# GpSimd subtracts two tiles at once and takes two residual sums; SyncE's queue and the first batch in another order

## What is computed

```python
x = x + layernorm(attention(layernorm(x)))
x = x + layernorm(ffn(layernorm(x)))

# attention, 16 heads of 8 columns, 512 positions
q, v = x @ Wq.T + bq, x @ Wv.T + bv
bits = ([q, 1] @ hyperplanes) >= 0                  # 6 bits, so 64 buckets
scores = q @ q.T / sqrt(128)
coeff = 62 + (bucket[s] == bucket[t])
out = softmax(scores * coeff) @ v

# feed-forward, 128 -> 512 -> 512 -> 512 -> 128, weights of -1, 0, 1 with a scale per output
h = silu(x @ w1 * s1) * (x @ w2 * s2)
h = gelu(h @ h1 * s);  h = gelu(h @ h2 * s);  out = h @ w3 * s3
```

## Time and profile before

| | us |
|---|---|
| median of three runs | 1542.07 (1539.42 to 1546.05) |
| the profiled execution, its own time | 1544.71 |
| its span in the profile | 1542.9 |
| first coefficients of batch 0 | at 40.42 |
| last tile of batch 0, of batch 15 | at 115.8, at 1454.6 |
| TensorE, VectorE busy | 1366.8, 1341.6 |
| GpSimd, ScalarE busy | 1241.5, 1184.0 |

### The profile page before, as it was taken

How to read it: one execution, slowest core, us unless ns; L and a number is a source line. 1 busy time by engine, 2 the same in 40 slices (tenths; PEclk the granted TensorE clock), 3 DMA queues, 4 the chain that set the end, 5 groups by cost and what they waited for, 6 DMA issues and landing times. The chain is left out here.

```text
span 1542.9 us, 22812 instructions
## 1 busy us (share of the span) xinstructions
PE 1366.8 (89%) x6502; PEld 630.4 (41%) x6624; DVE 1341.6 (87%) x4058; ACT 1184.0 (77%) x1587; POOL 1241.5 (80%) x1177
## 2 busy tenths in 40 slices
PE   2667899999989999898989989899998989899896
PEld 1222344353444434343443434444353444434343
DVE  3999999999999999999998989899999999898620
ACT  2465878888888888788888877878888788788731
POOL 1799988889888988888887888888889888888810
PEclk9987999999999999999999999999999999999999
DMA  2522321223132222312221221322213232222000
GB/s 59 151 70 66 76 64 53 70 47 87 44 77 72 60 62 60 81 36 76 73 70 50 57 75 47 76 69 51 72 43 84 52 76 66 52 61 57 16 0 14
DMA packets 145230, 95.44 MB, mean 62 GB/s; under 512 B 102608, under 2 KB 134608, under 8 KB 145104
## 3 DMA queue, kind: packets, MB, share of 16 engines
q1 hardware_dynamic: 145104, 93.97, 24.0%
HBM read 83.21 MB, written 10.75 MB: 61 GB/s over the span
## 5 line engine op out<-in xcount | busy, mean ns | idle before, releaser
L900 POOL TENSOR_TENSOR logits<-max_row,logits 128x512 f32<-128x512 f32 x912 | 1139.7, 1283 | 161.0 <-ACT max_row L930 156.3
L707 DVE CUSTOM_DVE_ANT_0 logits<-s_bank,coeff 128x512 f32<-128x512 f32 x1024 | 698.6, 682 | 0.2 <-issue 0.2
L688 DVE TENSOR_SCALAR coeff<-brow,bcol 128x516 bf16<-128x516 bf16 x1024 | 482.7, 471 | 70.3 <-PE s_bank L489 24.9
L939 ACT ACTIVATE probs<-logits 128x1024 f32<-128x1024 f32 x512 | 525.0, 1054 | 8.3 <-POOL logits L900 7.3
L489 PE MATMUL s_bank<-mov_stack,stat_stack 128*128 128x512 bf16 x902 | 325.9, 394 | 105.0 <-DVE rowmax L707 39.1
L489 PEld LDWEIGHTS s_bank<-mov_stack,stat_stack 128*128 128x128 bf16 x1024 | 95.6, 98 | 452.1 <-issue 206.7
L930 ACT COPY max_row<-s_bank 128x512 f32<-128x512 f32 x256 | 148.6, 580 | 166.4 <-PE s_bank L497 166.3
L518 PE MATMUL aux_bank<-probs,v_pad 128*32 128x512 f32 x2048 | 265.8, 615 | 6.8 <-issue 3.9
L622 PE MATMUL f_bank<-hid_a,h_sb 128*128 128x512 f32 x512 | 243.0, 596 | 14.1 <-DVE hid_a L805 12.1
L632 PE MATMUL f_bank<-hid_b,h_sb 128*128 128x512 f32 x512 | 249.3, 600 | 1.6 <-ACT hid_b L1014 1.4
L497 PE MATMUL s_bank<-ident,rowmax 128*128 128x128 f32 x1024 | 159.5, 280 | 8.0 <-issue 2.4
(11 more groups left out here) (83 smaller groups left out, 1132.7 us busy)
## 6 DMA issues: line engine op xcount, KB each, us to landing
brow<-bucket_scratch SPq DMA_DIRECT2D x64, 516.0 KB
mov_stack<-q_scratch SPq DMA_DIRECT2D x64, 288.0 KB
stat_stack<-q_scratch SPq DMA_DIRECT2D x192, 96.0 KB
q_scratch<-q_parts SPq DMA_DIRECT2D x48, 128.0 KB, 3.5
x_in<-in_x SPq DMA_DIRECT2D x16, 256.0 KB, 10.4
x_res<-in_x SPq DMA_DIRECT2D x16, 256.0 KB, 2.8
out<-ffn SPq DMA_DIRECT2D x16, 256.0 KB, 2.3
h_sb<-in_h1T SPq DMA_DIRECT2D x1, 1024.0 KB, 8.5
```

The lines of the kernel that those rows point to most:

```text
L688: nc.vector.tensor_scalar(coeff[:, k % 3, :].rearrange("p (r n) -> p r n", r=ROW_RUNS), brow[:, h // 4 % 2, h % 4, :, 0:RUN], bcol[:, b % ...
L707: nc.vector.tensor_tensor_reduce(out=logits[:, k % RING, :], in0=tile_bank(k)[:], in1=coeff[:, k % 3, 0:SEQ], scale=float(E) ** -0.5, scal ...
L900: nc.gpsimd.tensor_tensor(logits[:, k % RING, :], max_row[:, h % 2, :], logits[:, k % RING, :], ALU.subtract).then_inc(below_max_done, 1)
L939: nc.scalar.activation(probs[:, h // 4 % 2, h % 4, t:t + 2, :], logits[:, k % RING:k % RING + 2, :], ACT.Exp, scale=-1.0).then_inc(probs_d ...
```

## The change

GpSimd takes two neighbouring tiles of a head in one instruction, with `max_row` read twice. In the seven heads where VectorE takes the fourth tile, GpSimd takes a pair and a single tile. Both residual sums move from VectorE to GpSimd in the same slots. `apart` goes. SyncE's queue is written as a loop over slots: the store of q (now two DMAs, five parts in all, c0 c1 c2 c0 c1) stands in slot 1, the load of x in slot 2, the store of the bucket rows in slot 39 and `x_res` in slot 40; `mov_stack` is loaded in three DMAs of 24 rows and `stat_stack` in three of 24 rows that are read in a rotated order; the bucket rows are kept in DRAM with the pitch that they have in SBUF. For batch 0 the projections use PSUM banks of their own and fewer waits, and the query projection of batch 1 moves into slots 2 to 8 of batch 0.

```diff
+            for parts, row in ((PARTS, 0), (PARTS - 1, PARTS * DH)):
+                sp.dma_start(q_scratch[p][row:row + parts * DH, :].rearrange("(c d) (h n) -> (d h) c n", d=DH, h=H),
+                             q_parts[:, 0:parts, :]).then_inc(q_written, 16)
...
-                sp.dma_start(mov_stack[0:KROWS, slot].rearrange("p h n -> p (h n)"),
-                             q_scratch[b][:, cols].unsqueeze(0).broadcast_to([PARTS, PARTS * DH, 4 * SEQ])
-                             ).then_inc(stack_loaded[slot], 16)
                 for i in range(PARTS):
                     rows = slice(i * PARTS * DH, (i + 1) * PARTS * DH)
+                    sp.dma_start(mov_stack[rows, slot].rearrange("p h n -> p (h n)"),
+                                 q_scratch[b][0:PARTS * DH, cols]).then_inc(stack_loaded[slot], 16)
                     sp.dma_start(stat_stack[rows, slot].rearrange("p h n -> p (h n)"),
-                                 q_scratch[b][i * DH:(i + 1) * DH, cols].unsqueeze(0).broadcast_to(
-                                     [PARTS, DH, 4 * SEQ])).then_inc(stack_loaded[slot], 16)
+                                 q_scratch[b][i * DH:(i + PARTS) * DH, cols]).then_inc(stack_loaded[slot], 16)
...
                 if k == V_SLOT:
-                    pe.wait_ge(bits_done, p + 1)
+                    if begun(p):
+                        pe.wait_ge(bits_done, p + 1)
...
                 if k == PROJ_SLOT:
                     pe.wait_ge(q_done, p + 1)
-                    pe.wait_ge(q_part_steps, 4 * (p + 1))
+                    if begun(p):
+                        pe.wait_ge(q_part_steps, 4 * (p + 1))
...
-                if k == RESIDUAL_SLOT:
-
-                    dve.wait_ge(normed_done, f + 1)
-                    dve.wait_ge(x_res_loaded, 16 * (f + 1))
-                    nc.vector.tensor_tensor(y1[:, f % 2], y1[:, f % 2], x_res[:], ALU.add).then_inc(y1_done, 1)
...
                 h, t = divmod(k, ST)
-                if t == 0:
+                first = k - 1 if t % 2 else k
+                n = k - first + 1
+                if t < 2:
                     pool.wait_ge(max_row_done, b * H + h + 1)
                 pool.wait_ge(logits_done, b * TILES + k + 1)
-                nc.gpsimd.tensor_tensor(logits[:, k % RING, :], max_row[:, h % 2, :], logits[:, k % RING, :],
+                tiles = logits[:, first % RING:first % RING + n, :]
+                nc.gpsimd.tensor_tensor(tiles, max_row[:, h % 2, :].unsqueeze(1).broadcast_to([P, n, SEQ]), tiles,
                                         ALU.subtract).then_inc(below_max_done, 1)
...
+                    if feed and k == RESIDUAL_SLOT:
+
+                        pool.wait_ge(normed_done, f + 1)
+                        pool.wait_ge(x_res_loaded, 16 * (f + 1))
+                        nc.gpsimd.tensor_tensor(y1[:, f % 2], y1[:, f % 2], x_res[:], ALU.add).then_inc(y1_done, 1)
+                    if finish and k == Y2_SLOT:
+
+                        pool.wait_ge(end_normed_done, g + 1)
+                        nc.gpsimd.tensor_tensor(ffn[:], ffn[:], y1[:, g % 2], ALU.add).then_inc(y2_done, 1)
```

More of the change, by code:

```diff
@@ L43 @@
 PARTS = 3
+ROTATED = 2 * PARTS - 1
 KROWS = PARTS * PARTS * DH
@@ L49 @@
 PADDED = ROW_RUNS * RUN
+ROW_PITCH = ROW_RUNS * RUN_PITCH
 EPS = 1e-5
@@ L123 @@
 S_BANKS = 4
+Q_STORE_SLOT = 1
+FIRST_XNT_SLOT = 2
+FIRST_Q_STORE_SLOT = 11
+X_LOAD_SLOT = 2
+ROW_STORE_SLOT = 39
+X_RES_SLOT = 40
+OUT_SLOT = 63
 SHARED_HEADS = (0, 1, 5, 6, 8, 12, 15)
@@ L316, in maxima_bank, with projection_bank @@
             return s_bank[(k + (k + 1) // ST - 1) % S_BANKS]
-        POOL_TILES = TILES - len(SHARED_HEADS)
-        def pool_tiles(k):
-            return sum(not by_vector(n) for n in range(k + 1))
+        def projection_bank(p, n):
+            return aux_bank if begun(p) else f_bank[n]
         def quads_at(i, k, lag, attend, feed):
@@ L331, in quads_at, with query_at @@
             return []
+        def query_at(i, k, query):
+            steps = []
+            if query and not (i == -1 and k >= XNT_SLOT):
+                steps.append((i + 2, k))
+            if i == 0 and FIRST_XNT_SLOT <= k < FIRST_XNT_SLOT + TILES - XNT_SLOT:
+                steps.append((1, k - FIRST_XNT_SLOT + XNT_SLOT))
+            return steps
         def begun(b):
@@ L401, in iteration @@
                 p, b, f, g = i + 1, i, i - 1, i - 2
-                if query and project and not attend:
-                    sp.wait_ge(xnT_psum, p + 1)
-                    apart(sp)
-                    sp.dma_start(x_in[:], x_view[p + 1]).then_inc(x_loaded, 16)
-                if attend:
-                    if begun(b):
-                        sp.wait_ge(logits_done, b * TILES)
-                        apart(sp)
-                    load_stacks(b, 1)
-                    if query:
+                for k in range(TILES):
+                    if attend and k % QT == 0 and k // QT + 1 < QUADS:
+                        quad = k // QT + 1
+                        if begun(b) or quad > 1:
+                            sp.wait_ge(logits_done, b * TILES + (quad - 1) * QT)
+                        load_stacks(b, quad)
+                    if project and k == (FIRST_Q_STORE_SLOT if i == 0 else Q_STORE_SLOT):
+                        store_query(p)
+                    if query and project and k == (FIRST_Q_STORE_SLOT - 2 if i == 0 else X_LOAD_SLOT):
@@ L447, in iteration @@
-                if project:
-                    if attend:
-                        sp.wait_ge(logits_done, b * TILES + 3 * QT)
-                        apart(sp)
-                    load_stacks(p, 0)
-                if finish:
-                    store_output(g)
+                    if project and k == ROW_STORE_SLOT:
+                        store_row(p)
+                        if not attend:
+                            sp.wait_ge(q_written, 16 * Q_DMAS * (p + 1))
+                            sp.wait_ge(stacks_clear, 3)
+                            load_parts(p, 0)
@@ L456, in _ @@
+                    if finish and k == OUT_SLOT:
+                        store_output(g)
             stages(sp, iteration)
@@ L664, in iteration @@
                         transpose_output(b, quad)
-                    if query:
-                        query_step(i + 2, k, attend)
+                    for p, slot in query_at(i, k, query):
+                        query_step(p, slot, p > 1)
                     if project:
@@ L718, in moments @@
                     dve.wait_ge(stats_done, n)
-                    apart(dve)
                     for t in range(ST):
@@ L730, in output_step @@
                     dve.wait_ge(rden_done, b * QUADS + quad + 1)
+                    if quad == 0 and b:
+                        dve.wait_ge(normed_done, b)
                     nc.vector.tensor_tensor(
@@ L859, in iteration @@
                         project_step(i + 1, k)
-                    if query:
-                        query_step(i + 2, k)
+                    for p, slot in query_at(i, k, query):
+                        query_step(p, slot)
                     if finish:
```

117 lines of the change are left out of this document (55 added, 62 removed).

## The result

The changed kernel takes 1501.39 us (median of 4 runs, 1500.63 to 1502.52) against 1544.06 in the runs of before beside it (1539.42 to 1550.77): a ratio of 0.972, 95% interval 0.968 to 0.976. That is 42.7 us where 22.5 were forecast: the time lies at the lower edge of the range of 1501 to 1537, and outside the forecast's own 1511 to 1529. The runs of before lie 11 us apart, those of after 2; that turns out to matter.

A forecast was written before the change was run, and what follows sets the result against it. VectorE was taken to bound each batch's first half and TensorE the second; minus 18.8 (stalls), minus 4.3 (start) and plus 0.6 (end) gave minus 22.5, so 1519.5 us, range 1501 to 1537.

The forecast's parts named there:

- The stall of quad 3: VectorE's wait for quad 3's DMA load at its first coefficient in each batch; loading it ahead of `x_res` would remove it.
- The pairs: GpSimd's subtractions of two tiles at once: 2.38 us each forecast, valued at nothing for the end of the program.
- The sums: Two residual sums leaving VectorE in the half where TensorE sets the pace: value nothing, bound 2.9 us a batch.
- The wait of the statistics for GpSimd's sum: New wait of VectorE's statistics in slot 23: 0.35 us idle forecast, nothing to pay and no gain.
- The end: Last sum, on the path that ends the program, takes 1.28 in place of 0.69: plus 0.6 us.
- the term of minus 18.8: Steady batches: VectorE's waits for quad 3 in 15 batches go, each counted one for one, minus 18.8 us.
- The rival's sign: Rival on TensorE's clock: a denser TensorE is granted less clock, four more slow batches cost 10 us, 1530; chance 0.12.
- the saving of a pair: GpSimd: each of 25 pairs a batch saves about 0.17 us against two single subtractions, about 4 us less.
- The start: Ahead of the first tile: first coefficients at 33.1 in place of 40.4, minus 7.3 us; net minus 4.3 with batch 0.
- the early bound: Start: earliest case for the first tile, 29, with loads starting at 22.5 and 2 us to land.
- batch 1's q steps: Query projection steps of batch 1, now in slots 5 and 6 of batch 0: plus 3 us (1.4 to 5).
- The 4.9: Start: stacks moving at the full DMA rate land in 2.5 us in place of 7.4, 4.9 us less.

The follow-up runs named there:

- b_quad3_first: The kernel before, with only SyncE's queue reordered so that quad 3 is loaded ahead of the wait and load of `x_res`: 1516.11 us against 1540.63.
- a_single_tiles: The changed kernel with GpSimd subtracting tile by tile instead of in pairs, both residual sums left on GpSimd: 1503.33 us, ratio 0.975 to the kernel before.
- a_sums_vector: The changed kernel with both residual sums moved back from GpSimd to VectorE: 1502.97 us, ratio 0.975 to the kernel before.
- b_copy: The kernel before, run once more unchanged for a second profile: 1541.39 us.
- a_old_stack_loads: The changed kernel with mov and stat stacks loaded in the old form (three copies as outermost dimension), new queue order kept: 1506.42 us, ratio 0.978.

## Why the prediction was too small

**Right.** The stall of quad 3 goes, by the order of SyncE's queue alone (b_quad3_first). The pairs cost 2.37 us and the steady batch doesn't feel them (a_single_tiles). The sums are worth 0.16 us in a steady batch (a_sums_vector), near the nothing of the sum and far from its bound of 2.9. The wait of the statistics for GpSimd's sum is 0.15 or nothing in the steady batch, 0.35 forecast. The direction and the reason for the stall's going hold.

The end, 0.7 more where 0.6 was forecast, came out right by luck. The 0.6 is the last sum alone; by a_sums_vector the sums on GpSimd cost 2.8 there, and some other part of the change gives 2.1 back. Which one, no run shows. In after's chain of work that ended last, GpSimd's output sum stands ahead of its last subtractions, for which ScalarE's exponential waits until 1421.13:

```profile
1411.69 1.27 POOL ffn L921
1412.96 8.17 POOL logits L899 x4
1421.13 0.02 issue
1421.15 1.06 ACT probs L951
```

That delay of the batch behind it was no term of the sum.

**The step that failed** is the term of minus 18.8: "the stall adds to the batch one for one". It measured minus 28.1 in b_quad3_first. The 9.3 beyond the stalls can be laid out by batch, each less its stall against the same batch of b_quad3_first. The five with a dip behind their stall took 1.8, 2.9 and 2.9 more in the middle, and 1.6 and 1.5 in the last two (86.28 and 86.71 against 84.72 and 85.23), 10.7 in sum. The nine others from batch 2 on took 0.12 to 0.17 each, 1.3 in sum, which no dip explains. Batch 1 took 2.7 less (82.07 against 84.79); it has 84.82 in the second profile of before, so this is a difference between executions and not the queue's. Against that second profile (b_copy, three dips) batches 1 to 15 give 24.4, 18.7 of them stalls, which is near the 24.5 of the medians: the profile on which the forecast rested was a costly one. I had taken one for one from two batches and took the second for its long stall, 1.82, without looking at the clock behind it; it happened to be one of two long stalls without a dip. The batches near 825 to 1010 that took 91 to 92.5 were in my text, but as a rival: that a denser TensorE would be granted less clock. It was the other way about. The clock fell where TensorE had stood idle, so a change that fills its idle time wins the clock as well. The rival's sign was wrong, and those three batches were part of the gain. A smaller slip: the earlier trace rows call the wait that ends at 636.93 TensorE's last for VectorE before 691, but one of 0.21 ends at 637.53; it changes nothing. Nor does the saving of a pair, which by the prediction's own 2.57 and 2.38 is 0.19 and not 0.17.

The Trainium skill, in TensorE: Matmul & The Clock Gate, section "What's actually happening", says that the default state is throttled and activity releases it. Our rows agree in direction: 0.57 behind 2.14 us idle, 0.50 behind 4.92, 0.60 behind 3.36. That sentence gives the rival the other sign.

**The rest of the 35.5** is 7.4: 3.7 in batches 1 and 2, and 3.7 in batches 3 to 15, or 0.3 each in most (87.89 to 87.59). Of these 0.3 the sums are 0.16; the other 0.15 I can't assign to an edit. Batch 2 goes with the sums too: it takes 89.17 to 89.31, less the stall, in b_quad3_first and in both profiles of before, 89.81 in a_sums_vector, which keeps the new first batch, and 87.66 in after. So 1.5 more came from a term that the sum put at nothing. Why batch 2 gains more than a steady batch is open. Batch 1, of which TensorE runs a part at the low clock, takes 82.07 and 84.82 in the two profiles of before; its 2.2 can't be assigned.

In all the span fell 20.8 us further than forecast: 9.3 by the stalls' term, 7.4 by the rest of the batches, 4.2 by the start and batch 0.

**The start** gave 9.9 where I had 7.3, because two terms were mis-sized. SyncE's queue from 22.13, in after, shows the loads behind the store of the rows at 21.68 (22.1 forecast):

```profile
21.68 0.34 SPq L413 DMA_DIRECT2D bucket_scratch<-brow  x1
22.13 0.36 SPq L391 DMA_DIRECT2D mov_stack<-q_scratch  x1
...
24.52 0.35 SPq L400 DMA_DIRECT2D brow<-bucket_scratch  x1
```

Issue was over at 24.87 in place of 28.7: loads started 0.4 us ahead of the early bound, and the six took 2.35 us in place of the 4.3 at 0.72 each. Landing then took 5.65, more than the 4.4 that I had left. Batch 0 took 1.4 us more, the least of the 1.4 to 5 allowed for batch 1's q steps. No run takes these steps out, and the mean granted clock over batch 0 is 0.87 in after and 0.93 in before, so that they are the cause is not shown.

How many engines carry a load of 24 rows was the question on which I cited the Trainium skill. The window of after while such loads run, and below it the same microsecond of a_old_stack_loads, with the old form (DMA share before last, GB/s last):

```profile
24.00:25.00 1.00, 0.00 (x0) 0.00 (x0) 0.00 (x0) 0.00 (x0) 0.84 (x3) 1.00 0.75 184
```

```profile
24.00:25.00 1.00, 0.00 (x0) 0.00 (x0) 0.00 (x0) 0.00 (x0) 0.84 (x3) 1.00 0.19 45
```

0.75 of 16 is 12 engines, and 0.19, as in the earlier trace rows, is three. The rule of the Trainium skill, in DMA: Bandwidth & Descriptors, section on why a DMA increments its semaphore by 16 and not by 1, gives the same two numbers. The 4.9 that the prediction took from the rates in the earlier trace rows for this measured 5.2 (a_old_stack_loads).

## What to carry over

In this kernel a wait on the path had two prices: its length, and what TensorE lost behind it when its clock fell. Before pricing a stall, list every batch with its length less its stall and the granted clock behind it; a batch chosen as an example may be one of the lucky ones. Runs that scatter by 11 us, and equal batches that differ by 3, are a reason to look. And where two engines alternate in setting the pace, moving work of 0.7 us from the one half to the other (a number in a list) gave 7.5 us by the medians, about twice what pairing the subtractions (1.9) and moving the sums (1.6) gave together.

## Unexpected of the hardware

- TensorE's clock fell to half behind idle time of 2.14 us in one batch and stayed up behind 2.31 in another; 8 of 10 stalls of 1.48 us or more on VectorE brought it, none of 20 shorter ones. A second fall in two batches stood behind 1.76 us.
- One transfer of 24 rows is issued in 0.36 us, one with three copies as the outermost dimension in 0.72: six of the first cost less than the four that they replace.
- A GpSimd subtraction that reads one 512-column input twice, 1024 columns in all, costs no more a column than the plain one: 2369 ns, against 2380 from the line through 198 and 1283. Beside it VectorE's instructions stay as long as they were (L695 472 ns, L714 683; 471 and 682 before).
